# Layer 0's first expert product with the weights stationary and the tokens moving

## The reference, cut to what matters

```python
gate = jax.nn.silu(jnp.einsum('td,edf->tef', xf, gate_w))   # d = 256, f = 512
up = jnp.einsum('td,edf->tef', xf, up_w)
h = gate * up
out = jnp.einsum('te,tef,efd->td', w, h, down_w)            # w: the weight of each expert, per token
```

## Time and profile before

| | |
|---|---|
| median of three runs | 805.38 us (804.9 to 805.58) |
| span of the profiled execution | 803.3 us (its own device time isn't given; the median less the span is 2.1 us) |
| TensorE busy | 707.5 us, 88% |
| VectorE / ScalarE / GpSimd busy | 472.0 / 374.7 / 355.7 us |
| layer 0's experts | from about 140 to 364 us of the span |

### The profile page before, as it was taken

How to read it: one execution, slowest core, us unless ns; L and a number is a source line. 1 busy time by engine, 2 the same in 40 slices (tenths; PEclk the granted TensorE clock), 3 DMA queues, 4 the chain that set the end, 5 groups by cost and what they waited for, 6 DMA issues and landing times.

```text
span 803.3 us, 16716 instructions
## 1 busy us (share of the span) xinstructions
PE 707.5 (88%) x5182; PEld 568.7 (71%) x5183; DVE 472.0 (59%) x1213; ACT 374.7 (47%) x881; POOL 355.7 (44%) x310
## 2 busy tenths in 40 slices
PE   3988960899999999997988999589999999999991
PEld 2757950466666666665877988478888888888871
DVE  4898798643433333335789897946544545554540
ACT  5797557333333333333455764724344344344430
POOL 3429980123222322220666874034555556555331
PEclk9997995899999999997999999789999999999996
DMA  9970044041211121115312234512232333232335
GB/s 267 413 290 1 1 142 148 27 114 27 37 27 26 28 38 26 26 20 158 100 53 79 81 99 141 182 41 41 47 46 47 53 53 49 44 47 45 40 35 149
DMA packets 37177, 66.02 MB, mean 82 GB/s; under 512 B 3776, under 2 KB 29360, under 8 KB 35568
## 3 DMA queue, kind: packets, MB, share of 16 engines
q1 hardware_dynamic: 23696, 46.90, 17.6%
q0 software_dynamic: 13248, 18.21, 14.4%
q10 hardware_dynamic: 192, 0.38, 0.1%
HBM read 44.83 MB, written 23.35 MB: 85 GB/s over the span
## 4 chain that ended last, share of the span: by engine, by line
PE 70%; DVE 16%; ACT 5%; DMA 3%; issue 2%; POOL 2%; POOLq 0%; SPq 0%; DVEq 0%
PE PS L788 15%; PE PS L981 15%; PE PS L994 15%; PE PS L806 8%; PE PS L1349 3%; PE PS L796 3%; DVE tops L734 2%; PE PS L1376 1%; ACT Y L2000 1%; PE PS L966 1%; DMA Y<-in_wtok_dram 1%; DVE h L2504 1%; PE PS L2151 1%; POOL X L1598 1%; PE PS L1357 1%
## 5 line engine op out<-in xcount | busy, mean ns | idle before, releaser
L788 PE MATMUL PS<-X,Y 128*128 x576 | 133.7, 382 | 1.1 <-DVE Y L886 1.1
L1160 POOL DMA_INDIRECT sum<-X,dest x45 | 88.5, 1967 | 96.9 <-ACT X L1063 81.4
L994 PE MATMUL PS<-X 128*128 x720 | 125.7, 273 | 1.9 <-ACT X L1063 1.9
L981 PE MATMUL PS<-X 128*128 128x256 f16 (+1 forms) x768 | 122.6, 265 | 0.7 <-issue 0.7
L1053 ACT ACTIVATE X<-PS,X 128x256 f32<-128x256 f32 (+1 forms) x192 | 72.8, 463 | 103.3 <-PE PS L981 100.2
L952 POOL DMA_INDIRECT sum<-Y,dest x24 | 38.1, 1586 | 148.3 <-ACT Y L863 148.3
L897 DVE SCALAR_TENSOR_TENSOR Y<-PS,Y 128x512 f32<-128x512 f32 x48 | 36.1, 751 | 111.4 <-PE PS L788 111.2
L981 PE MATMUL PS<-X,Y 128*128 128x256 f16 (+1 forms) x384 | 100.1, 264 | 0.0
L788 PEld LDWEIGHTS PS<-X,Y 128*128 128x128 f16 x576 | 56.8, 99 | 60.3 <-issue 3.5
L994 PE MATMUL PS<-Y,X 128*128 x360 | 98.2, 273 | 0.0
L981 PEld LDWEIGHTS PS<-X 128*128 x768 | 71.8, 97 | 10.7 <-issue 1.3
(11 more groups left out here) (398 smaller groups left out, 1410.2 us busy)
## 6 DMA issues: line engine op xcount, KB each, us to landing
X<-in_w_dram SPq DMA_DIRECT2D x11, 1024.0 KB, 16.6
stage<-in_w_dram SPq DMA_DIRECT2D x16, 512.0 KB, 3.6
sum<-h SPq DMA_DIRECT2D x2, 2048.0 KB, 7.6
xs<-Y SPq DMA_DIRECT2D x2, 1040.0 KB, 5.6
xs<-Y SPq DMA_DIRECT2D x2, 1032.0 KB, 6.0
h<-in_txt_dram SPq DMA_DIRECT2D x2, 1024.0 KB, 17.2
Y<-in_patches_dram SPq DMA_DIRECT2D x3, 672.0 KB, 8.2
sum<-h SPq DMA_DIRECT2D x2, 768.0 KB, 6.3
```

The source lines that it names most:

```text
L788: ins = nc.tensor.matmul(PS[:, 2 * u + s, 0:F0], x_[:, slot, k, :], w_[:, at_:at_ + F0], start=(n == 0), stop=(n == 3 * KC - 1))
L981: ins = nc.tensor.matmul(PS[:, 2 * s + c // 2, (c % 2) * T1:(c % 2) * T1 + tokens], part[:, off:off + P], x_[:, slot, k, 0:tokens], start= ...
L994: ins = nc.tensor.matmul(PS[:, 4 + a, 0:D], h_[:, s, c, a * P:(a + 1) * P], part[:, off:off + D], start=(s == 0 and c == 0 and n == 0), st ...
L1160: nc.gpsimd.indirect_dma_start(out=sum1, out_offset=bass.IndirectOffsetOnAxis(ap=dest[:, i:i + 1], axis=0), in_=y1buf[:, u % 2, i - first_ ...
```

## The change

- `products_in`: the weights are stationary, 128 columns of them, and the 128 tokens move. For each s there are 2 (gate, up) x 4 (blocks of 128 hidden) x 6 = 48 matmuls of 128 columns in place of 12 of 512. The result has the hidden index on partitions, which is what `product_out` wants, so `transpose_h` is gone.
- The expert weight of a row can't be applied there any longer. VectorE multiplies gate and up alone, and the weights are applied to the outputs: `product_out` writes one bank for each expert (4 and 5), ScalarE copies the first times its weight (`first_y`), VectorE adds the second times its weight (`whole_y`).
- `dve_scale` and the row weights (now multiplied by the common scale) come before the first `combine`; TensorE's order in a tile is products_in(i,0), transpose_x(i+1), product_out(i-1,1), products_in(i,1), product_out(i,0).
- The preparation of attention's weights uses bank 6 in place of 5; an unused semaphore is gone.

```diff
             def products_in(i, s, w_, slot):
-                for u in range(2):
-                    n = 0
-                    for k in range(KC):
-                        off = in_w0(s * W0N + (u * KC + k) * F0)
-                        for x_, at_ in ((xh, off), (xh, off + CW), (xl, off)):
-                            ins = nc.tensor.matmul(PS[:, 2 * u + s, 0:F0], x_[:, slot, k, :], w_[:, at_:at_ + F0],
...
+                for u, done in ((0, gate_psum), (1, up_psum)):
+                    for c in range(F0 // P):
+                        n = 0
+                        for k in range(KC):
+                            off = in_w0(s * W0N + (u * KC + k) * F0 + c * P)
+                            for x_, at_ in ((xh, off), (xl, off), (xh, off + CW)):
+                                ins = nc.tensor.matmul(PS[:, 2 * u + s, c * P:(c + 1) * P], w_[:, at_:at_ + P], x_[:, slot, k, :],
...
-            def transpose_h(i, s):
...
             def product_out(i, s, w_):
                 pe.wait_ge(hT_lo, 2 * i + s + 1)
-                if s == 0:
-                    wait_from(pe, y_copied, i)
+                wait_from(pe, y_copied if s else y_begun, i)
...
-                        ins = nc.tensor.matmul(PS[:, 6, 0:D], h_[:, s, c, :], w_[:, at_:at_ + D],
+                        ins = nc.tensor.matmul(PS[:, Y_BANKS[s], 0:D], h_[:, s, c, :], w_[:, at_:at_ + D],
...
-                    transpose_h(i - 1, 1)
                 if not known(i, SLOT0 - 1):
                     transpose_x(i + 1, 1 - slot, j + slot)
                 if not known(i, 0):
-                    product_out(i - 1, 0, last)
+                    product_out(i - 1, 1, last)
                 products_in(i, 1, w_, slot)
-                transpose_h(i, 0)
-                if not known(i, 0):
-                    product_out(i - 1, 1, last)
+                product_out(i, 0, w_)
...
+            def first_y(i, slot, j):
+                act.wait_ge(y_half, i + 1)
+                act.wait_ge(x_w, i + 1)
                 if not (isinstance(j, int) and j == 0):
                     act.wait_ge(y_out[slot], 16 * j)
+                nc.scalar.activation(ybuf[:, slot, :], PS[:, Y_BANKS[0], 0:D], ACT.Copy, scale=wall[:, bass.ds(i, 1), 0])\
+                    .then_inc(y_begun, 1)
...
+                nc.vector.tensor_tensor(hh[:, s, :], PS[:, 2 + s, 0:F0], sg[:, s, :], ALU.mult).then_inc(h_ready, 1)
...
+            def whole_y(i, slot):
+                dve.wait_ge(y_done, i + 1)
+                dve.wait_ge(y_begun, i + 1)
+                part = ybuf[:, slot:slot + 1, :]
+                nc.vector.scalar_tensor_tensor(out=part, in0=PS[:, Y_BANKS[1], 0:D].unsqueeze(1),
+                                               scalar=wall[:, bass.ds(i, 1), 1], in1=part, op0=ALU.mult, op1=ALU.add)\
+                    .then_inc(y_copied, 1)
...
+                if not known(i, SLOT0 - 1):
+                    split_x(i + 1, 1 - slot)
+                    row_weights(i + 1, 1 - slot, j + slot)
                 combine(i, 0)
...
+                split_h(i, 0)
                 if not known(i, 0):
-                    split_h(i - 1, 1)
...
+                    whole_y(i - 1, 1 - slot)
                 combine(i, 1)
-                split_h(i, 0)
+                split_h(i, 1)
```

More of the change, by code:

```diff
@@ L396, in build @@
         std_ready = sem("std_ready")
-        nega_ready = sem("nega_ready")
         patch_normed = sem("patch_normed")
@@ L432, in build @@
         h_ready = sem("h_ready")
-        hT_psum = sem("hT_psum")
+        y_half = sem("y_half")
         hT_hi = sem("hT_hi")
@@ L436, in build @@
         y_done = sem("y_done")
+        y_begun = sem("y_begun")
         y_copied = sem("y_copied")
@@ L511, in build @@
         O_BANKS = (4, 5, 0, 6)
+        Y_BANKS = (4, 5)
         block = ctx.enter_context(nc.Block())
@@ L782, in products_in @@
                     pe.wait_ge(x_lo, i + 1)
-                for u in range(2):
-                    n = 0
-                    for k in range(KC):
-                        off = in_w0(s * W0N + (u * KC + k) * F0)
-                        for x_, at_ in ((xh, off), (xh, off + CW), (xl, off)):
-                            ins = nc.tensor.matmul(PS[:, 2 * u + s, 0:F0], x_[:, slot, k, :], w_[:, at_:at_ + F0],
-                                                   start=(n == 0), stop=(n == 3 * KC - 1))
-                            n += 1
-                    ins.then_inc(up_psum if u else gate_psum, 1)
@@ L793, in transpose_h @@
-            def transpose_h(i, s):
[L794 to L797, removed]
+                for u, done in ((0, gate_psum), (1, up_psum)):
[5 more added lines that the diff above has]
+                                ins = nc.tensor.matmul(PS[:, 2 * u + s, c * P:(c + 1) * P], w_[:, at_:at_ + P], x_[:, slot, k, :],
+                                                       start=(n == 0), stop=(n == 3 * KC - 1))
+                                n += 1
+                    ins.then_inc(done, 1)
@@ L799, in product_out @@
             def product_out(i, s, w_):
                 pe.wait_ge(hT_lo, 2 * i + s + 1)
-                if s == 0:
-                    wait_from(pe, y_copied, i)
-                for c in range(4):
+                wait_from(pe, y_copied if s else y_begun, i)
+                for c in range(F0 // P):
                     off = in_w0(s * W0N + 2 * KC * F0 + c * D)
                     for n, (h_, at_) in enumerate(((hTh, off), (hTh, off + CW), (hTl, off))):
-                        ins = nc.tensor.matmul(PS[:, 6, 0:D], h_[:, s, c, :], w_[:, at_:at_ + D],
-                                               start=(s == 0 and c == 0 and n == 0), stop=(s == 1 and c == 3 and n == 2))
@@ L808, in product_out @@
-                if s == 1:
-                    ins.then_inc(y_done, 1)
+                        ins = nc.tensor.matmul(PS[:, Y_BANKS[s], 0:D], h_[:, s, c, :], w_[:, at_:at_ + D],
+                                               start=(c == 0 and n == 0), stop=(c == F0 // P - 1 and n == 2))
+                ins.then_inc(y_done if s else y_half, 1)
             def weights(i):
@@ L836, in pe_experts0 @@
             n = SLOT0 - 1
[L837 to L840, removed]
+            product_out(n, 1, weights(n))
         def act_experts0(act):
@@ L854, in split_h @@
                     act.wait_ge(scale_ready, 1)
-                act.wait_ge(hT_psum, 2 * i + s + 1)
-                nc.scalar.activation(hTh[:, s, :, :].rearrange("p c r -> p (c r)"), PS[:, 4 + s, 0:F0], ACT.Copy,
+                act.wait_ge(h_ready, 2 * i + s + 1)
+                nc.scalar.activation(hTh[:, s, :, :].rearrange("p c r -> p (c r)"), hh[:, s, :], ACT.Copy,
                                      scale=hscale[:, 0:1]).then_inc(hT_hi, 1)
-            def copy_y(i, slot, j):
-                act.wait_ge(y_done, i + 1)
+            def first_y(i, slot, j):
+                act.wait_ge(y_half, i + 1)
+                act.wait_ge(x_w, i + 1)
@@ L861, in copy_y, with tile @@
                 if not (isinstance(j, int) and j == 0):
                     act.wait_ge(y_out[slot], 16 * j)
-                nc.scalar.activation(ybuf[:, slot, :], PS[:, 6, 0:D], ACT.Copy, scale=hscale[:, 1:2])\
+                nc.scalar.activation(ybuf[:, slot, :], PS[:, Y_BANKS[0], 0:D], ACT.Copy, scale=wall[:, bass.ds(i, 1), 0])\
+                    .then_inc(y_begun, 1)
+            def tile(i, slot, j):
+                if known(i, 0):
+                    split_x(0, 0)
+                if not known(i, 0):
+                    first_y(i - 1, 1 - slot, j + slot - 1)
+                nonlinear(i, 0)
+                if not known(i, SLOT0 - 1):
+                    split_x(i + 1, 1 - slot)
+                split_h(i, 0)
+                nonlinear(i, 1)
+                split_h(i, 1)
@@ new lines, in act_experts0, with dve_experts0, split_x, row_weights @@
+            pipelined(act, SLOT0, tile)
+            n = SLOT0 - 1
+            first_y(n, n % 2, n // 2)
+        def dve_experts0(dve, chain):
+            def split_x(i, slot):
+                dve.wait_ge(x_hi, i + 1)
+                nc.vector.tensor_tensor(xl[:, slot].rearrange("p k r -> p (k r)"), PS[:, 7, 0:KC * P],
+                                        xh[:, slot].rearrange("p k r -> p (k r)"), ALU.subtract).then_inc(x_lo, 1)
+            def row_weights(i, slot, j):
+                dve.wait_ge(x_in[slot], 16 * (j + 1))
+                nc.vector.tensor_scalar(wall[:, bass.ds(i, 1), :], xin[:, slot:slot + 1, D:PAY0], hscale[:, 1:2], None, ALU.mult)\
+                    .then_inc(x_w, 1)
+            def combine(i, s):
+                step = 2 * i + s + 1
+                dve.wait_ge(up_psum, step)
+                dve.wait_ge(act_out, step)
+                nc.vector.tensor_tensor(hh[:, s, :], PS[:, 2 + s, 0:F0], sg[:, s, :], ALU.mult).then_inc(h_ready, 1)
+            def split_h(i, s):
+                dve.wait_ge(hT_hi, 2 * i + s + 1)
```

(34 more changed lines are left out.)

6 lines of the change are left out of this document (3 added, 3 removed).

## The result

The changed kernel takes 875.95 us in the median (873.41 to 878.19, four runs); the kernel before, run beside it, took 805.14. The ratio is 1.0888, with a 95% interval of [1.0864, 1.0912]: 71 us slower. The forecast was 883 us, with a range from 861 to 903.

A forecast was written before the change was run, and what follows sets the result against it. The array bounded the kernel before; afterwards TensorE's sequencer would: products 8.8, product_out 2.0, group number loads 1.2 and the rest 0.3 make 12.3 us a tile against 8.9. With the ends, the stage grows 78 us: 883 us, range 861 to 903.

The forecast's parts named there:

- the sequencer's account: Layer 0 tiles: TensorE's sequencer becomes the bound, with 80 register instructions a tile at 125 ns; 12.3 us against 8.9.
- Products: The first product's 96 matmuls a tile, paced by the sequencer at 0.092 us each: 8.8 us, floor 8.0, ceiling 9.2.
- The starved runs of layer 1: Two L981 stretches with the sequencer behind, 3.39 us for 36 matmuls, 94 ns each; basis for the first product's pace.
- product_out and its lead: Second product: 2.6 us a tile on the array, sequencer needs 2.0, the 0.6 ahead spent next; net 2.0, ceiling 2.3.
- Loads and the rest: Per tile: group number loads, now exposed, 1.2 us; token transposes, waits and the loop's jump 0.3 us.
- Edits at nothing: VectorE and ScalarE steps, output buffers, preparation bank and dropped semaphore: claimed to fit in the 12.3 us tile at no cost.
- The ends: Stage start and finish: tile 1 at 155.8, products_in(23,1) ends at 437.1, tail 5.1 us against 8.7; stage 78 us longer.
- A, the array's account: Rival: TensorE's array still sets the pace at 56 ns a matmul, 8.2 us a tile, 789 us in all; chance 0.07.
- B: Rival: first product's weight loads can't overlap, 97 ns each, 12.1 us a tile, 879 us in all; chance 0.07.
- C, the fallen clock: Rival: gaps in TensorE's work halve its granted clock, 15.8 us a tile, about 960 us in all; chance 0.04.

The follow-up runs named there:

- Experiment 1: Changed kernel with layer 0's weights always group 0's at fixed addresses, without register instructions or group number loads in this stage: 785.9 us, ratio 0.9768 to the kernel before.
- experiment 2: Control: the kernel before with the same fixed weights of group 0 in layer 0: 802.94 us, ratio 0.9987 to the kernel before.
- experiment 3: Changed kernel with fixed weights in the first product alone, group numbers still loaded and used by the second product: 788.4 us, ratio 0.9795 to the kernel before.
- experiment 5: Changed kernel with the first product's k = 1 weights fixed for both experts, so fixed and register addresses alternate every three matmuls: 794.61 us, ratio 0.9883.
- experiment 6: Changed kernel with product_out(i-1,1) using the current tile's group, so two group number loads a round in place of three: 868.37 us, ratio 1.0784.
- Experiment 7: Kernel before, first product and transposes kept, but one output bank per expert and expert weights applied at the copies: 804.95 us, ratio 0.9989.
- experiment 9: Changed kernel with the group chosen by branching among four copies of a tile's TensorE code, in place of register addresses: 1051.2 us, ratio 1.3077.

## Why the prediction was right, point by point

The step that decided was the sequencer's account: 80 register instructions a tile, 125 ns a piece. Experiment 1 takes them away and the kernel goes to 785.9 us, 90 us down; experiment 2 shows that this is not a gain by itself; experiment 3 puts it on the first product's 64; experiment 5 shows that it isn't the number alone. The trace of the changed kernel closes the account: from one jump of the loop (313.17) to the next (337.55) the sequencer goes from instruction to instruction without a stop. By the distances of their starts a tile is 8.19 us of the first product's register instructions, 2.06 of product_out's, 1.07 of loads of the number and 0.88 of all else, 12.2 in all.

- **Products.** Forecast 8.8 us a tile (8.0 to 9.2), measured 4.07 and 4.01 (308.14 to 312.15): 8.1. The starved runs of layer 1 held more of the longer steps: the 16 register instructions under the run of 24 step by 134 ns on average, with single steps of 182 and 215, and 0.1 us for a wait instruction falls into its 2.24 us; here the mean step is 128. I had lowered 94 ns to 92; it is 85. The term is 0.6 to 0.7 us too large.
- **product_out and its lead.** 1.33 us on the array each (306.81 to 308.14), and 2.06 a tile of sequencer time against my net 2.0.
- **Loads and the rest.** Forecast 1.2 + 0.3. A load takes the sequencer 0.71 us (0.77 by experiment 6), so 1.1 a tile; the 1.2 holds. What I called the rest is 0.88 us, not 0.3: I had priced it by the array's 0.22 us of transposes, but the sequencer also has a wait and an address to reckon before each product_out, 0.2 us a time. This term is too small by 0.6, and the products too large by as much. That the sum came out at 12.3 against 12.2 is luck in the size; the mechanism isn't touched by it.
- **Edits at nothing.** Experiment 7 confirms the second bank and the weights at the copy. From 150 to 430 us the trace has no wait of TensorE for VectorE or ScalarE.
- **The ends.** The timeline after, answering to the earlier trace rows:

```profile
155.43 2.75 PE L791 MATMUL PS<-Y,X 128*128 128x128 f16 x31 [0.20 <-issue]
```
```profile
429.60 4.08 PE L791 MATMUL PS<-Y,X 128*128 128x128 f16 x48
...
436.11 1.50 PE L803 MATMUL PS<-X,Y 128*128 x12 [0.92 <-DVE Y L893]
...
438.40 1.56 POOL L953 DMA_INDIRECT sum<-Y,dest  x1 [5.64 <-DVE Y L902]
```

Tile 1 starts at 155.4 (155.8 forecast). products_in(23,1) ends at 433.7 (437.1 forecast) and the last send starts 4.7 us after it (5.1 forecast; 8.7 before). The send is 74.0 us later than the 364.35 of the earlier trace rows, the span 73.1 longer: the rest of the kernel shifted as it was. The forecast's surplus, 78 less 74, is for the most part that of the 23 tiles. The other 3 us between 883 and 875.95 are no term of the prediction's: the rest of the kernel took 1 us less, and the profiled execution, at 878.19 us, was the longest of the four.

- **The rivals.** A, the array's account, failed only in its condition. Where the condition is made true (experiments 1 and 3) it comes to 785.9 and 788.4 us, against its 789. B is out by experiment 1. C, the fallen clock, didn't occur in the changed kernel, at 1.00; experiment 9 shows a granted clock of 0.50 after the array has stood for 11 us. The Trainium skill ("TensorE: Matmul & The Clock Gate", section "Back-to-back issue gap") gives 81 ns for a sustained pair of load and matmul of 128 columns. That is near the 85 ns measured in the changed kernel, but as a rate of the pair it doesn't hold here: the pairs run at 56 ns when their addresses are fixed.

## What to carry to other kernels

Where matmul operands are addressed through a register, count the address changes, not only the columns: in this kernel each costs TensorE's sequencer about 125 ns, and a form with short matmuls and many weight blocks is bound by that while the array's own sum still promises a gain. Look for stretches of the same line that run at two paces; here the faster one was paid from the sequencer's lead. That lead is short, 17 matmuls at most in these traces, so spread such work evenly, and turn round only as much as the room carries.

## What was not expected

- The lead of the sequencer can't be saved up over 2.7 us: with the same 48 register instructions a tile takes 10.27 us when those of the first product stand in one piece, and 8.60 when they are spread out.
- Branches on TensorE's sequencer into copies of a tile's code: 2.2 us each in the median, 4.1 at most; with the loop's jump, 11 us of standstill before a tile.
